# Layer 3's local-attention masks written by 64x64 quarters, and eight slots with other step orders

## The reference

```python
x = x + 0.5 * ffn(_layernorm(x))     # the feed-forward part of layer 0, 1, 2 or 3
x = x + attn(_layernorm(x))          # attention of that layer
x = x + 0.5 * ffn(_layernorm(x))
```

```python
sim = jnp.einsum('bhwid,bhwjd->bhwij', bq, bk)      # 64 queries x 128 keys per window
mask = (i < j) | (i > j + WINDOW) | (j == -1)       # j == -1: no window before the first
sim = jnp.where(mask, -jnp.finfo(sim.dtype).max, sim)
attn = jax.nn.softmax(sim, axis=-1)
```

## Time and profile before

| | us |
|---|---|
| median of 3 runs | 2942.89 |
| lowest and highest | 2940.99, 2950.08 |
| the profiled execution | 2941.67 |
| its span, first to last instruction | 2939.9 |
| around the span | 1.8 |

### The profile page before, as it was taken

The page is one execution under the profiler, slowest core; times in us unless marked ns, Lnnn a source line. Parts: engine busy times, 40 slices in busy tenths (PEclk is TensorE's granted clock), DMA queues, the critical chain, the costliest instruction groups (busy, mean ns, idle before and its releaser), DMA issues.

```text
span 2939.9 us, 63499 instructions
## 1 busy us (share of the span) xinstructions
PE 2544.9 (87%) x24589; PEld 1617.3 (55%) x24589; DVE 2167.9 (74%) x5133; ACT 1664.1 (57%) x4036; POOL 787.8 (27%) x810
## 2 busy tenths in 40 slices
PE   6878889788898888988877988999988889989998
PEld 3556666554455544547755875565653222556655
DVE  4856557778887668877567567888877777888883
ACT  2334443466642367753476546767747666676773
POOL 1010001111111111121332246546511114455650
PEclk9879998899999999999999999999989998999999
DMA  3623420000000000014600661010100000001001
GB/s 114 243 41 57 81 62 1 1 1 1 1 1 1 1 1 1 1 58 168 252 6 1 216 217 30 15 28 17 28 3 3 1 1 13 16 16 28 18 19 28
DMA packets 123078, 131.95 MB, mean 45 GB/s; under 512 B 81941, under 2 KB 101653, under 8 KB 121242
## 3 DMA queue, kind: packets, MB, share of 16 engines
q1 hardware_dynamic: 120250, 122.70, 14.0%
q0 software_dynamic: 2048, 4.20, 0.4%
q10 hardware_dynamic: 480, 0.98, 0.1%
HBM read 80.73 MB, written 29.04 MB: 37 GB/s over the span
## 4 chain that ended last, share of the span: by engine, by line
PE 45%; DVE 27%; ACT 10%; issue 7%; POOL 5%; DMA 2%; SPq 0%; DVEq 0%; POOLq 0%; ACTq 0%
DVE nm L1251 6%; PE ps L1210 4%; PE ps L586 3%; PE ps L1990 3%; PE ps L1187 3%; PE ps L2199 3%; PE ps L1151 3%; PE ps L2365 2%; ACT hand L550 2%; PE ps L663 2%; PE ps L439 2%; DVE pre L2285 2%; PE ps L2502 2%; POOL ss L2276 1%; PE ps L265 1%
## 5 line engine op out<-in xcount | busy, mean ns | idle before, releaser
L1251 DVE TENSOR_REDUCE nm<-ps 128x2 f32<-128x256 f32 (+2 forms) x704 | 424.0, 636 | 65.3 <-PE ps L1151 42.4
L1300 ACT ACTIVATE core<-ps 128x512 f32<-128x512 f32 x672 | 358.7, 591 | 93.0 <-PE ps L1192 48.4
L380 POOL TENSOR_TENSOR rstd<-ve,weights 128x4 f32<-128x4 f32 x80 | 83.0, 1038 | 879.5 <-DVE ve L357 828.1
L2271 POOL TENSOR_TENSOR pre<-pre,sin 128x512 f32<-128x512 f32 x128 | 231.2, 1825 | 226.9 <-ACT pre L2242 200.1
L1151 PE MATMUL ps<-hand 128*128 128x128 bf16 (+4 forms) x1024 | 246.0, 314 | 44.9 <-DVE nm L1251 39.8
L550 ACT COPY hand<-ps 64x512 bf16<-64x512 bf16 x336 | 194.7, 579 | 132.1 <-PE ps L586 81.7
L1187 PE MATMUL ps<-hand 128*128 128x128 bf16 (+4 forms) x1024 | 225.3, 307 | 21.7 <-ACT hand L550 15.1
L2405 ACT ACTIVATE core<-ps,nm 128x128 f32<-128x128 f32 x512 | 181.9, 379 | 67.0 <-DVE nm L2422 66.0
L2276 POOL TENSOR_TENSOR ss<-ss,weights 128x16 f32<-128x16 f32 x64 | 196.6, 3072 | 71.6 <-DVE ss L2291 69.9
L2199 PE MATMUL ps<-weights,pre 128*128 128x512 f32 x384 | 200.0, 624 | 11.2 <-ACT hand L2253 6.6
L1261 POOL CAST hand<-nm 128x16 bf16<-128x16 f32 x192 | 59.0, 308 | 492.6 <-DVE nm L1251 484.3
(11 more groups left out here) (352 smaller groups left out, 6313.6 us busy)
## 6 DMA issues: line engine op xcount, KB each, us to landing
hand<-in_experts SPq DMA_DIRECT2D x48, 836.0 KB, 4.7
shear<-post SPq DMA_DIRECT2D x64, 256.0 KB
core<-in_experts SPq DMA_DIRECT2D x12, 836.0 KB, 5.1
core<-shear SPq DMA_DIRECT2D x128, 64.0 KB, 2.2
hand<-hand SPq DMA_DIRECT2D x16, 512.0 KB, 4.4
hand<-hand SPq DMA_DIRECT2D x16, 384.0 KB, 5.6
core<-in_stream SPq DMA_DIRECT2D x2, 2048.0 KB, 7.7
shear<-pre SPq DMA_DIRECT2D x16, 256.0 KB
```

The source lines that it names most:

```text
L1251: nc.vector.tensor_reduce(nm_of(unit), src, AX.X, ALU.max, negate=True).then_inc(negmax, 1)
L1300: nc.scalar.activation(prob8[:, i % PROBS, 0:w], m.ps[:, RING[at % NR], 0:w], ACT.Exp).then_inc(ring_out, 1)
L2271: ins = nc.gpsimd.tensor_tensor(o[:, :, :, z:z + hl], x[:, :, :, y0:y0 + hl], sn[:, t, :, z:z + hl].unsqueeze(2).to_broadcast([P, 2, LH, h ...
```

## The change

It has two parts. In `l3_layer_core` each mask product becomes two, one for each head's rows and columns: a 64x64 corner of the identity times 64 rows of the mask. They write the same values at the same places, with as many columns as before. In eight slots (5, 6, 8, 17, 29, 32, 39, 44) the strings for TensorE, VectorE and ScalarE are other interleavings of the same steps, and in five of them (5, 6, 17, 32, 39) GpSimd's too. No step is added or taken away, the number of fillers in slots 5, 6 and 17 stays at 96, 119 and 99, and SyncE's strings stay as they are.

```diff
@@ -2351,12 +2351,18 @@
                     left(pe, "score banks")
                 if i >= 2:
                     pe.wait_ge(exps, 4 * (i - 1))
+                heads = [slice(64 * e, 64 * e + 64) for e in range(2)]
                 if half == 0:
-                    nc.tensor.matmul(out[:, 0:P], m.identb, m.negfirst, start=True, stop=True)
-                    nc.tensor.matmul(blocks(out)[:, 1:4, :], m.identb, m.negwin.unsqueeze(1).to_broadcast([P, 3, P]),
-                                     start=False, stop=True, skip_group_check=True)
+                    for rows in heads:
+                        nc.tensor.matmul(out[rows, 0:P], m.identb[rows, rows], m.negfirst[rows, :], start=True, stop=True)
+                    for rows in heads:
+                        nc.tensor.matmul(blocks(out)[rows, 1:4, :], m.identb[rows, rows],
+                                         m.negwin[rows, :].unsqueeze(1).to_broadcast([64, 3, P]),
+                                         start=False, stop=True, skip_group_check=True)
                 else:
-                    nc.tensor.matmul(out, m.identb, m.negwin.unsqueeze(1).to_broadcast([P, 4, P]), start=True, stop=True)
+                    for rows in heads:
+                        nc.tensor.matmul(blocks(out)[rows], m.identb[rows, rows],
+                                         m.negwin[rows, :].unsqueeze(1).to_broadcast([64, 4, P]), start=True, stop=True)
                 for r in range(4):
                     n = 4 * half + r
                     lo, at = (0, WIN) if n == 0 else (keys(n), 0)
```

Strings of the eight slots, in part:

```diff
@@ slot 5 @@
-     "vector": "b4c1b1a1c1b3a1c1b1a4b1a3b1a4b1a1c1a3b1a7c1b1",
-     "scalar": "b9a2b1a2b1a2b1a2c1a1b1a2b2a1b1a8",
+     "vector": "b4c1a3b1c1b2c1a1b2a5b1a1c1a1b1a1b1a3b1a6b1a3c1",
+     "scalar": "b5a1b5a3b1a2b1a2c1a1b2a2b2a9",
...
@@ slot 8 @@
-    {"tensor": "b1c1b2c1b6a2b2a3b1a1b1a2b1c1a2b1c1a2c1a1b1a8b1c1b2",
-     "vector": "b4c1b3c1b1a4c1a2c1a1b1a1b3c1b1",
+    {"tensor": "c1b1c1b1c1b7c1b2a3b2a3b1a2c1b1a2c1a2b1a1b1a8b2",
+     "vector": "b4c4b5a7b1a1b2c1b1",
...
@@ slot 17 @@
-     "gpsimd": "b1d1a1b6"},
+     "gpsimd": "a1b6d1b1"},
...
@@ slot 29 @@
-    {"tensor": "a4b1a1b1a7b1a1b1a4b1c2a3c1a2c2a6c1b4",
-     "vector": "b3a2b1a3b1a1b1a1b1a1b7a1b1a3b1a1b4a1b2a2b4c5",
-     "scalar": "b2a2b1a1b1a15c1b4",
+    {"tensor": "a4c1b1a3b1a1c1a6b1a1b1c1a2b1c1a1c1a10c1b4",
+     "vector": "b3a2b1a5c1b1a1b2a1b7a2b1a2c1a1b7a2b4c3",
+     "scalar": "b2a3b2a4c1a11b4",
...
@@ slot 32 @@
-    {"tensor": "a2b1a1b1a1b2a1b1a1b2a1b7a1b2a1b3a2b2",
-     "scalar": "a1b1a2b2a2b2a1b2a1b6a1b5a2b3",
+    {"tensor": "a2b4a2b2a1b2a2b5a1b5a3b3",
+     "scalar": "a1b4a3b3a2b6a1b4a3b4",
...
@@ slot 39 @@
-     "vector": "b4a2c1a3c5a1c1b7a1b2a1b2a1b1c2b1c1a1b1c1a1c1b1",
-     "scalar": "a2b1a1b1a1b1a1b2c1a1c1b2c1a1b1c1a2b1c1b1a1b2",
+     "vector": "b3a1b1a1c2a1c2a1c2a1c1b4a1b3a1b2a1b2a1b1c1b1c1a1c1b1c1a1c1b1",
+     "scalar": "a1b3a3b2a1c2a2b3c2a1b1a1c1b1a1b2",
...
@@ slot 44 @@
-     "vector": "b5a2c1b1a1b1c1b1a1c1b3a1b1a1b3c1a1b4a1b1a1b1a2c1",
+     "vector": "b5a2c1b2a2b4c1a2b3c1b1a1b3c1b1a1b1a2b1a1c1",
...
```

More of the change, by code:

```diff
@@ L2589 @@
      "sync": "a4b5"},
-    {"tensor": "b1c1a1b1e2c1e1b1e5b1e3b1e1a1e2a1e2c1e24b1e9b1e9b1e7a1e3b1e2a3b1a1c1e3b1e2a2b1e2a1e3b1e1c1e3a1e1b1a2b"
-               "1a1b1c1b1a3e1a2e5a3e5a1",
-     "vector": "b4c1b1a1c1b3a1c1b1a4b1a3b1a4b1a1c1a3b1a7c1b1",
-     "scalar": "b9a2b1a2b1a2b1a2c1a1b1a2b2a1b1a8",
-     "gpsimd": "b6d1",
-     "sync": "a4b5"},
[L2596 to L2600, removed]
+    {"tensor": "b1c1b1e3b1a1b1e3b1c1e1a1c1e4a2e10c1e2b1e17b1e1b1e1a1e10b1e5a1b1e7a1e3b1a1e7b1c1e1a2e2b1a1e2a1e2b1c1b"
+               "1a1e1b1a2b1a2e7a1e1a1e4a2e1a3e1",
+     "vector": "b4c1a3b1c1b2c1a1b2a5b1a1c1a1b1a1b1a3b1a6b1a3c1",
+     "scalar": "b5a1b5a3b1a2b1a2c1a1b2a2b2a9",
+     "gpsimd": "b3d1b3",
+     "sync": "a4b5"},
+    {"tensor": "c1b1a2b1e4b1e6b1c1b1e14a2e25c1e11b1e1a1c1b1e9c1b1a3e1b1e2c1e3b1e4a1b1a2e3b1e9a1e4b1a2e1b1e3a1b1a1e1b"
+               "1a1e1b1e10a2e2a2e1a1e1a2e3",
+     "vector": "b4c1a6b1c1b3a1b1a1c2a1b1a3b1a3b1a3b1c1a5b1a1",
+     "scalar": "b5a2b4a2c1b1a2b1a3b1a2b3a1b1a8",
+     "gpsimd": "b2d1b4",
      "sync": "a4b5"},
@@ L2607 @@
      "sync": "a4"},
-    {"tensor": "b1c1b2c1b6a2b2a3b1a1b1a2b1c1a2b1c1a2c1a1b1a8b1c1b2",
-     "vector": "b4c1b3c1b1a4c1a2c1a1b1a1b3c1b1",
-     "scalar": "b11a2c1a1",
+    {"tensor": "c1b1c1b1c1b7c1b2a3b2a3b1a2c1b1a2c1a2b1a1b1a8b2",
+     "vector": "b4c4b5a7b1a1b2c1b1",
+     "scalar": "b11a1c1a2",
      "gpsimd": "b1d1",
@@ L2655 @@
      "gpsimd": "b1a1c1b5c1b1d1"},
[L2656 to L2659, removed]
-     "gpsimd": "b1d1a1b6"},
+    {"tensor": "e1c1e1c1b1a1b1a1e3b1a1e2b1a1b1a2e6a1e9a1e17a1e3c1e3c1e8a2e8a1e1b1e6b1e8b1e1a1e1b1a1e1b1a2b1a1e1b1e10"
+               "b1e2b1e7a1",
+     "vector": "b4a6b4a1b5a1b6a1b2a2b3a2b1a3b1c1a1b1",
+     "scalar": "b6a1b3a1b2a1b3a1",
+     "gpsimd": "a1b6d1b1"},
     {"tensor": "e2a1c1a1b1e4b1a1b1a1b1a1b1a2e5a1c1e2a1c1e11a1e4c1e1a1e17a1e1b1e1a1b2e1a1b1e1a1e1b1e1a1e1b1e4b1a1b1a1"
@@ L2729 @@
      "sync": "a14b1a2"},
-    {"tensor": "a2b1a1b1a1b2a1b1a1b2a1b7a1b2a1b3a2b2",
-     "vector": "b3a1b2a2c1a1b2a1b1a1b3a1b4a1b1c1b4a2b1a1",
-     "scalar": "a1b1a2b2a2b2a1b2a1b6a1b5a2b3",
-     "gpsimd": "b1c2b9d1b3",
+    {"tensor": "a2b4a2b2a1b2a2b5a1b5a3b3",
+     "vector": "b3a1b2a1b2a2b3a1b1a1b1a1b3a1c1b1c1b3a2b2a1",
+     "scalar": "a1b4a3b3a2b6a1b4a3b4",
+     "gpsimd": "b1c1b3c1b3d1b6",
      "sync": "b1"},
@@ L2764 @@
      "sync": "c1b1"},
-    {"tensor": "c1a1c1a1b1c2a1b1a1b1a1b1a1b1c2a1c2a2b1c1b1a1b1c1b2c1a1b1c1b2",
-     "vector": "b4a2c1a3c5a1c1b7a1b2a1b2a1b1c2b1c1a1b1c1a1c1b1",
-     "scalar": "a2b1a1b1a1b1a1b2c1a1c1b2c1a1b1c1a2b1c1b1a1b2",
-     "gpsimd": "b1c1b1d1b4",
+    {"tensor": "c1a1c1a1b1c1b1c1b1a1b1a2b1c1a1c1a2c3b1a1b2a1c1b1a1b1c1b1c1b2",
+     "vector": "b3a1b1a1c2a1c2a1c2a1c1b4a1b3a1b2a1b2a1b1c1b1c1a1c1b1c1a1c1b1",
+     "scalar": "a1b3a3b2a1c2a2b3c2a1b1a1c1b1a1b2",
+     "gpsimd": "d1b1c1b5",
      "sync": "c1"},
@@ L2788 @@
      "sync": "b1"},
-    {"tensor": "b1a2b2c1a1c1b2a1c1b2a1b3a1b1c1b1a1b2c1b3a1b1c1a3b3",
-     "vector": "b5a2c1b1a1b1c1b1a1c1b3a1b1a1b3c1a1b4a1b1a1b1a2c1",
-     "scalar": "b1a1b2a2b2a1b3a1b3a1b4c1b1a1b2a3b3",
+    {"tensor": "b1a2b1c1b1c1a2b5a2c1b5a1c1b3a1b2c2b1a3b2",
+     "vector": "b5a2c1b2a2b4c1a2b3c1b1a1b3c1b1a1b1a2b1a1c1",
+     "scalar": "b1a1b2a2b3a2b5a1b3a1b3c1b1a3b3",
      "gpsimd": "b12d1b1",
```

## The result

| | before | after |
|---|---|---|
| median, us | 2942.89 | 2925.01 |
| lowest and highest of 5 runs each | 2940.99, 2950.08 | 2922.66, 2929.50 |
| profiled execution, its span | 2941.67, 2939.9 | 2923.95, 2922.0 |
| PE, DVE busy, us | 2544.9, 2167.9 | 2527.4, 2163.8 |
| mean granted clock | 0.947 | 0.948 |

The ratio is 0.9942, with a 95% interval of 0.9927 to 0.9957: faster, by 12.6 to 21.5 us. Measured once more beside the experiments, the changed kernel took 2924.81 us against 2942.06, ratio 0.9953 (0.9939 to 0.9966). I had forecast 2930, range 2919 to 2944.

The account below looks back on a forecast made before the run. No engine bounds the kernel alone; in most edited slots chains of waits, set by the orders, do. From 2941.67 us, 10.3 for orders and 2.5 for masks leave 2928.9; the median standing 1.2 higher, 2930, range 2919 to 2944.

Parts of the forecast that it names:

- The sum: Whole kernel: 2941.67 us less 10.3 for orders and 2.5 for masks, median 1.2 above the profiled execution: 2930 us.
- Masks: Layer 3's mask units: quarters side by side, fewer array-size changes save 3.4 us of TensorE time, taken as 2.5.
- the sum is zero: At 111 masks behind a whole-array product, 0.10 us is paid before the mask instead of after: no gain.
- Slot 5: Three core steps of VectorE go into its 7.42 us stall before the split: 4 us (0 to 8.3).
- Slot 8: Post's three later divisions go ahead of VectorE's stall, its TensorE products into the first stretch: 2.5 us.
- Slot 29: Two post divisions early end TensorE's 3.08 us wait; the sorted tokens' load caps the gain: 2.5 us (0 to 2.8).
- Slot 32: Three pre steps in a row on ScalarE start the second projection's copy 3 us sooner: 3 us (0 to 5).
- Slot 39: VectorE makes post's normalised values before the core's fifth unit, but waits for shift DMAs: 1.5 us (-2 to 3).
- Slots 6, 17 and 44: Slot 6, short stalls: 0.5 us; slot 17, post's products ahead of pre's first: 1; slot 44, VectorE bounds it: 0.5.
- The third given back: Of the slots' 15.5 us a third is given back, the next chain being close behind; 10.3 kept.
- (B): Waits only change places as another input ends the stalls: 2937 us, no change to be told; 24%.
- (D): Orders wrong for real durations, steps ahead of their input hold queues, as in slots 39 or 17: 2948 to 2956 us; 9%.

Follow-up runs that it names:

- the early division: The changed kernel with VectorE's third division of slot 29 ahead of the four sorting steps: 2925.25 us against 2940.06 for the kernel before, ratio 0.9940.
- masks alone: The kernel before with only the masks by quarters, all orders as before: 2938.42 us against 2941.43, ratio 0.9996.
- orders alone: The kernel before with only the new strings of the eight slots, masks of the whole array: 2933.14 us against 2941.43, ratio 0.9970.
- masks twice: The changed kernel with every quarter of a mask issued twice: 2940.11 us against 2942.06 for the kernel before, ratio 0.9998.

## Why the prediction was right, and where it was off

**The sum** held, 12.8 us forecast for 13.8 to 17.9 measured; its terms were off in both directions.

**Masks.** That the quarters run side by side, and that units behind scores lose both changes of size, was right (0.25 us forecast, 0.25 measured). The step that failed is "the sum is zero" behind the whole array. I took the first load for uncovered on either side of the mask, but behind a quarter the scores' load is covered, 0.03 us in each of 107 units. Of the 6.8 us some 4 arrive, by the nine slots of steady clock; that is more than my 2.5 and than the upper end of 3.4 that I gave. The timed runs can't confirm it (3.0 by medians, 1.2 by the ratio).

**Slot 5.** The mechanism was right: three core steps in the stall, no stall over 5 us before L486. The size was not: 2.4 by the traces, 3.0 by the times, for 4.

**Slot 8** failed. I read TensorE's idle 4.0 us as room. The post's products did move into the first stretch, but TensorE was full there already (before it is busy for 5.00 us in each of the two windows from 415 to 425), so the second ranks came later by what the end got shorter: the stall before L850 ended 21.4 us into the slot before and 24.3 after, and 2.9 us of stall remained. Idle time at one place is no room for steps put at another. The take also left the clock out: what is behind the stall runs at 1.2 GHz, and the same order held at 2.4 GHz by fillers takes 31.0 us, near the 32 of the forecast. Whether the old order would be as short at that clock was not seen.

**Slot 29.** Forecast 2.5, capped by the load at 2.8; the traces say 1.7. Two things were off. The 3.08 us stall of the earlier trace rows did not go; it moved to another division, still behind the sort (3.54 above). And the cap came closer: counted from the last weight load of slot 28 the load is issued 0.6 us later than before (38.25 for 37.64) and takes 6.0 us where I had taken 5.4, so of 2.8 us some 1.6 were left, and L1851 starts 1.5 sooner (44.31 for 45.85). That it is "ended by the load" is not what the row shows: L1851 has no idle time before it, L720 and the load end within 0.1 us of each other, and in the second trace of the changed kernel the load is landed 0.4 us before L1851 starts. Both chains are level there. That the stall could go with nothing won is what the early division shows.

**Slot 32.** ScalarE, kernel after:

```profile
1768.78 0.58 ACT L2161 COPY pre<-ps 64x511 f32<-64x511 f32 x1
1770.64 0.59 ACT L2242 COPY pre<-ps 128x512 f32<-128x512 f32 x1 [1.28 <-PE ps L2199]
1771.12 0.60 ACT L2245 ACTIVATE pre<-ps 128x512 f32<-128x512 f32 x1
1771.61 0.59 ACT L2242 COPY pre<-ps 128x512 f32<-128x512 f32 x1
```

The second L2242 starts 2.8 us behind L2161, in the earlier trace rows 5.9: three us sooner as forecast, and 2.5 to 2.9 of the take of 3 arrived.

**Slot 39.** The wait that the change adds was short. SyncE, then VectorE, kernel after:

```profile
2132.02 0.75 SPq L2480 DMA_DIRECT2D post<-y  x1
...
2134.32 0.87 DVE L348 BATCH_NORM_STATS2 st<-post 128x6 f32<-128x128 f32 x4 [1.07 <-DMA post<-y]
```

The last shift is landed 1.6 us behind its issue, not 5.4, and costs VectorE 1.07. The gain is 1.9 with slot 40, for 1.5.

**Slots 6, 17 and 44.** 6 and 17 came within 0.4 of the takes. In 44 I took VectorE's 41.0 of 45.4 us for a bound, but its busy time fell to 37.5 with no step less: its four L2285 take 1.23 us each after and 2.25 before, with GpSimd's L2271 beside them both times. The cause is open; a busy time that can shrink is no bound. The slot gave 1.1 for 0.5, with old masks. **The third given back** was right in size: of 15.5 taken, 8 to 11 were measured. In part that is luck: the reason given, a next chain close behind, is seen in slot 29 alone, and the largest miss is slot 8.

**Rivals.** (B) has its mark in slots 8 and 29, where the stall only changed its place, not in the sum. (D) did not happen in these strings, but those of slot 5 with VectorE's old one show its price: 5 to 7 us in one slot.

## What to carry to other kernels

Before a step is moved into a stall, look at the queue at the place where it will stand: steps moved into a stretch in which that engine is full push everything behind them. When one releaser of a stall is removed, compute when the next input is there, a load above all, since that alone is the gain. For differences of under 0.5%, compare each stage over many traces and look for stages whose code is the same: how much they differ is the error of a single trace.

## What the runs showed of the hardware

- The granted clock falls at other places from execution to execution of one kernel. Over 177 runs of the kernels here the mean clock of a run was 0.941 to 0.952, and within a kernel a clock higher by 0.001 went with a time shorter by 1.6 us. In the two traces of the changed kernel slot 8 lasts 34.1 and 35.3 us, slot 15 74.3 and 72.7. At equal clock, by that slope, masks alone is 4.0 us under before and orders alone 8.2, with some 1.4 of uncertainty each; a change that itself moves the clock isn't fairly judged so.
- In slot 8's old order with fillers the clock fell to 1.2 GHz at 430 us, though TensorE had been busy for 4.43 us of the 5 before it, with fillers until 427.7 and then mostly products of one column. In the new order with fillers it was busy for 5.00 of the same 5 us, with fillers from 428.5 to 432.2, and the products of one column from 434 to 438 us ran at 2.4 GHz.
- A change from the whole array to 64x64 quarters costs some 0.10 us: a whole mask takes 0.31 us to its scores, and a further pair of quarters 0.21 in masks twice. The first load comes on top, by estimate 0.03 us in bf16 (the start of the scores' load behind the mask's) and 0.05 in 32 bits (what two changes leave of the 0.25 saved behind scores). With a bf16 product first in the new size, the 32-bit load was done under it.
- Of 27 us added to TensorE's time in layer 3's mask units 0.4 to 0.65 arrived at the end; of 6.8 us saved some 0.6, by an estimate from nine slots.
